# Graph layer in split precision: half of the third batch multiplied whole, and GpSimd's part of the split put in another order

## The reference

```
h   = relu(layernorm(x))                        # 512 x 128
HW_r = h @ W[r, :128] + (W_edges[r] @ W[r, 128:])   # seven relations r
out = max over r of A_r @ HW_r, with A_r in (A, A, roll, A^T, A^T, roll^T, identity)
x   = x + out + b
```

## Time and profile before

| | |
|---|---|
| median of 3 runs | 208.48 us (208.31 to 209.1) |
| the profiled execution | 208.36 us |
| its span in the profile | 206.6 us |
| TensorE busy | 198.2 us (96%), granted clock 1.00 |
| VectorE busy | 178.8 us (87%) |
| ScalarE busy | 162.3 us (79%) |
| GpSimd busy | 130.0 us (63%) |
| mean DMA rate | 247 GB/s |

### The profile page before, as it was taken

One profiled execution on the slowest core, in us unless ns is written; L12 is line 12 of the kernel. 1 busy time (PEld: TensorE's weight loads), 2 busy tenths in 40 slices (PEclk: granted clock), 3 DMA queues, 4 the chain that ended last, 5 costly groups with the idle time before them and its releaser, 6 DMA issues.

```text
span 206.6 us, 3426 instructions
## 1 busy us (share of the span) xinstructions
PE 198.2 (96%) x922; PEld 152.2 (74%) x922; DVE 178.8 (87%) x411; ACT 162.3 (79%) x432; POOL 130.0 (63%) x166
## 2 busy tenths in 40 slices
PE   6999999799999999999999999999999999999991
PEld 6556468568788787878878787877878786887871
DVE  3587869999889998999889998999989999997565
ACT  3987989597979969696997969698896969685230
POOL 4140246969593977939594696919695486959600
PEclk9999999999999999999999999999999999999999
DMA  6999999987896959699795969779695969923201
GB/s 183 311 360 361 361 359 270 304 268 224 312 293 187 387 127 392 153 336 263 244 351 140 389 126 368 218 257 342 210 352 100 396 136 295 261 91 47 65 2 51
DMA packets 33747, 51.07 MB, mean 247 GB/s; under 512 B 1872, under 2 KB 11328, under 8 KB 33728
## 3 DMA queue, kind: packets, MB, share of 16 engines
q1 hardware_dynamic: 31152, 46.53, 66.2%
q0 software_dynamic: 2304, 4.20, 13.1%
q10 hardware_dynamic: 272, 0.13, 0.2%
HBM read 46.65 MB, written 4.19 MB: 246 GB/s over the span
## 4 chain that ended last, share of the span: by engine, by line
PE 70%; DMA 11%; DVE 6%; SPq 4%; POOL 3%; issue 3%; ACT 0%; DVEq 0%; ACTq 0%; POOLq 0%
PE bank_p L846 10%; PE bank_p L847 8%; PE bank_p L848 8%; DMA x_bias<-in_biasT_dram 8%; PE bank_g L809 5%; PE bank_g L811 5%; PE bank_g L817 5%; PE bank_gT L800 5%; PE bank_gT L794 5%; PE bank_gT L791 5%; DMA x_bias<-in_xT_dram 4%; PE bank_p L836 3%; PE bank_p L733 3%; PE bank_p L741 2%; DVE best L632 2%
## 5 line engine op out<-in xcount | busy, mean ns | idle before, releaser
L330 POOL TENSOR_TENSOR a_lo<-adj_sb,a_hi 128x512 fp32r<-128x512 f32 x28 | 36.1, 1310 | 38.0 <-DVE h_lo L601 36.9
L337 POOL TENSOR_TENSOR aT_lo<-adjT_sb,aT_hi 128x512 fp32r<-128x512 f32 x28 | 39.5, 1575 | 0.0
L632 DVE TENSOR_TENSOR best<-bank_p,best 128x512 f32<-128x512 f32 x48 | 33.2, 691 | 5.8 <-PE bank_p L848 4.7
L414 ACT ACTIVATE a_hi<-adj_sb 128x512 fp32r<-128x512 f32 x56 | 34.5, 620 | 0.0
L423 ACT ACTIVATE aT_hi<-adjT_sb 128x512 fp32r<-128x512 f32 x56 | 34.4, 620 | 0.0
L629 DVE SCALAR_TENSOR_TENSOR best<-bank_p,c_col,best 128x512 f32<-128x512 f32 x32 | 23.9, 748 | 5.0 <-ACT best L472 4.4
L595 DVE TENSOR_TENSOR aT_lo<-adjT_sb,aT_hi 128x512 fp32r<-128x512 f32 x28 | 25.4, 945 | 0.0
L435 ACT ACTIVATE h<-x_sb,shift,rstd 128x128 f32<-128x128 f32 x60 | 24.6, 488 | 0.0
L323 POOL TENSOR_TENSOR o_sb<-best,x_bias 128x512 f32<-128x512 f32 x15 | 20.8, 1384 | 3.4 <-DMA x_bias<-in_xT_dram 3.4
L846 PE MATMUL bank_p<-hT_hi,w_hi 128*128 128x512 f32 x48 | 20.1, 420 | 0.4 <-ACT sumsT L465 0.4
L588 DVE TENSOR_TENSOR a_lo<-adj_sb,a_hi 128x512 fp32r<-128x512 f32 x28 | 20.3, 765 | 0.0
(11 more groups left out here) (118 smaller groups left out, 493.9 us busy)
## 6 DMA issues: line engine op xcount, KB each, us to landing
adj_sb<-in_adj_dram SPq DMA_DIRECT2D x15, 1024.0 KB, 5.5
adjT_sb<-in_adjT_dram SPq DMA_DIRECT2D x15, 1024.0 KB, 7.1
x_bias<-in_biasT_dram SPq DMA_DIRECT2D x16, 256.0 KB, 4.8
x_bias<-in_xT_dram POOLq DMA_DIRECT2D x16, 256.0 KB, 5.1
x_sb<-in_x_dram SPq DMA_DIRECT2D x15, 256.0 KB, 7.9
out_dram<-o_sb SPq DMA_DIRECT2D x15, 256.0 KB, 4.1
adj_sb<-in_adj_dram SPq DMA_DIRECT2D x4, 256.0 KB, 4.4
adjT_sb<-in_adjT_dram SPq DMA_DIRECT2D x4, 256.0 KB, 4.8
```

What stands on the lines that cost most here:

```text
L330: nc.gpsimd.tensor_tensor(a_lo[q][:, c, :], adj_sb[q][:, c, :], a_hi[q][:, c, :].bitcast(F32), ALU.subtract).then_inc(alo_last_ready, 1)
L337: nc.gpsimd.tensor_tensor(aT_lo[q][:, c, :], adjT_sb[q][:, c, :], aT_hi[q][:, c, :].bitcast(F32), ALU.subtract).then_inc(aTlo_last_ready, 1)
L414: nc.scalar.activation(a_hi[q][:, c, :], adj_sb[q][:, c, :], ACT.Copy, accum_out=sums[q][:, 0, c:c + 1]).then_inc(ahi_ready, 1)
L632: op = nc.vector.tensor_tensor(best[q][:, :], product, best[q][:, :], ALU.max)
```

## The change

In batch 2, chunks 2 and 3 of both aggregations are multiplied whole in fp32, and chunks 0 and 1 in three passes as before. GpSimd makes no low parts for batch 2. It runs `part_sums(2)` and `add_bias(2)` ahead of its loop, and starts to split at batch 3. In the loop `finish(b - 1)` waits for VectorE's low parts of `aT` of batch b, the split of `a` waits for VectorE's low parts of `a` of the same batch, and `add_bias` goes behind `part_sums`. ScalarE takes `std_of(b + 2)` behind the high parts of `gT` and `hT`. The counts in the loads' waits follow, and the loads also wait for the high parts.

```diff
@@ load_adj, and load_adjT with aThi, aTlo, aTlo_last @@
                 if b >= 2 + FIRST:
+                    sp.wait_ge(ahi_ready, (b - 1 - FIRST) * NS)
                     sp.wait_ge(alo_ready, (b - 1 - FIRST) * ND)
-                    sp.wait_ge(alo_last_ready, (b - 1 - FIRST) * NG)
+                if b > 2 + FIRST:
+                    sp.wait_ge(alo_last_ready, (b - 2 - FIRST) * NG)
@@ gpsimd @@
             add_bias(1)
-            for b in range(1, B):
-                if b >= 2:
-                    finish(b - 1)
+            part_sums(2)
+            add_bias(2)
+            for b in range(2, B):
+
+                pool.wait_ge(aTlo_ready, (b - FIRST + 1) * ND)
+                finish(b - 1)
                 if b + 1 < B:
 
+                    pool.wait_ge(alo_ready, (b - FIRST + 2) * ND)
                     pool.wait_ge(hlo_ready, b - FIRST + 2)
                     split_adj_last(b + 1)
-                    add_bias(b + 1)
                     split_adjT_last(b + 1)
                     part_sums(b + 1)
+                    add_bias(b + 1)
@@ scalar @@
                 if 2 <= b < B - 1:
                     split_adj(b + 1)
+                split_gT(b)
+                split_hT(b)
                 if 2 <= b < B - 2:
                     std_of(b + 2)
-                split_gT(b)
-                split_hT(b)
                 if b + 1 < B:
                     make_h(b + 1)
@@ tensor @@
+            def split_chunks(b):
+
+                return range(ND if b == FIRST else C)
+
             def aggregate_T(b):
                 q = b % 2
                 pe.wait_ge(hhi_ready, b - FIRST + 1)
                 pe.wait_ge(gTlo_ready, b)
-                for c in range(C):
+                if b == FIRST:
+                    pe.wait_ge(adj_in[q], times(b))
+                    for c in range(ND, C):
+                        nc.tensor.matmul(bank_gT[:, 0:N], h[q][:, c, :], adj_sb[q][:, c, :],
+                                         start=(c == ND), stop=False)
+                for c in split_chunks(b):
                     pe.wait_ge(ahi_ready, (b - FIRST) * NS + c + 1)
-                    nc.tensor.matmul(bank_gT[:, 0:N], h_hi[q][:, c, :], a_hi[q][:, c, :], start=(c == 0), stop=False)
+                    nc.tensor.matmul(bank_gT[:, 0:N], h_hi[q][:, c, :], a_hi[q][:, c, :],
+                                     start=(c == 0 and b > FIRST), stop=False)
...
```

More of the change, by code:

```diff
@@ L237, in load_adjT @@
                 if b >= 2 + FIRST:
+                    sp.wait_ge(aThi_ready, (b - 1 - FIRST) * NS)
                     sp.wait_ge(aTlo_ready, (b - 1 - FIRST) * ND)
-                    sp.wait_ge(aTlo_last_ready, (b - 1 - FIRST) * NG)
+                if b > 2 + FIRST:
+                    sp.wait_ge(aTlo_last_ready, (b - 2 - FIRST) * NG)
                 sp.dma_start(adjT_sb[q][:, :, :], adjT_dram[b]).then_inc(adjT_in[q], 16)
@@ L798, in aggregate_T @@
                     else:
-                        pe.wait_ge(alo_last_ready, (b - FIRST) * NG + c - ND + 1)
+                        pe.wait_ge(alo_last_ready, (b - FIRST - 1) * NG + c - ND + 1)
                     last = nc.tensor.matmul(bank_gT[:, 0:N], h_hi[q][:, c, :], a_lo[q][:, c, :],
-                                            start=False, stop=(c == C - 1))
+                                            start=False, stop=(c == split_chunks(b)[-1]))
                 last.then_inc(gT_psum, 1)
@@ L806, in aggregate @@
                 pe.wait_ge(best_done, b * NBEST)
-                for c in range(C):
+                if b == FIRST:
+                    pe.wait_ge(adjT_in[q], times(b))
+                    for c in range(ND, C):
+                        nc.tensor.matmul(bank_g[:, 0:N], h[q][:, c, :], adjT_sb[q][:, c, :],
+                                         start=(c == ND), stop=False)
+                for c in split_chunks(b):
                     pe.wait_ge(aThi_ready, (b - FIRST) * NS + c + 1)
-                    nc.tensor.matmul(bank_g[:, 0:N], h_hi[q][:, c, :], aT_hi[q][:, c, :], start=(c == 0), stop=False)
-                for c in range(C):
+                    nc.tensor.matmul(bank_g[:, 0:N], h_hi[q][:, c, :], aT_hi[q][:, c, :],
+                                     start=(c == 0 and b > FIRST), stop=False)
+                for c in split_chunks(b):
                     nc.tensor.matmul(bank_g[:, 0:N], h_lo[q][:, c, :], aT_hi[q][:, c, :], start=False, stop=False)
-                for c in range(C):
+                for c in split_chunks(b):
                     if c < ND:
@@ L815, in aggregate @@
                     else:
-                        pe.wait_ge(aTlo_last_ready, (b - FIRST) * NG + c - ND + 1)
+                        pe.wait_ge(aTlo_last_ready, (b - FIRST - 1) * NG + c - ND + 1)
                     last = nc.tensor.matmul(bank_g[:, 0:N], h_hi[q][:, c, :], aT_lo[q][:, c, :],
-                                            start=False, stop=(c == C - 1))
+                                            start=False, stop=(c == split_chunks(b)[-1]))
                 last.then_inc(g_psum, 1)
```

## The result

The changed kernel takes 205.41 us (median; 205.12 to 206.52) where the kernel before, timed beside it, takes 208.47. The ratio is 0.9864, with a 95% interval of 0.983 to 0.9898. So it is faster by 1.4%, 3.1 us. The forecast was 205.7 us with a range of 205.0 to 206.9. The profiled execution took 205.48 us with a span of 203.7.

The account below looks back on a forecast made before the run. TensorE's own work was taken to bound the kernel, beside its waits. 208.36 us less 1.91 in batch 2 and 0.88 in later batches gave 205.57, as a median 205.7; range 205.0 to 206.9 us.

Parts of the forecast that it names:

- the two pools: TensorE time to gain beyond its own work: 2.99 us in batch 2 and 0.88 us spread over later batches.
- Items 1 and 3: Batch 2: without GpSimd's split VectorE's pair falls from 3.49 to 1.29 us; the batch takes 12.88, a gain of 1.91.
- Item 2: Batch 2 on TensorE: four whole chunks cost 0.82 us, the passages between split and whole 0.26, together 1.08.
- Items 4 to 6: GpSimd's early part_sums and add_bias and its new loop order cost nothing; all 12 later batches become clean, gaining 0.88 us.
- item 5: GpSimd's order in a clean batch: finish runs T + 3.6 to T + 4.9, just missing VectorE; 1.4 us in hand.
- Item 7: ScalarE's std behind hT_hi leaves sumsT 0.11 us in hand; TensorE's wait taken as 0, bound 1.4 us.
- Rival A: sumsT late for TensorE through std's new place: 0.05 us in 11 batches costs 0.55, giving 206.2 us; chance 0.20.
- Rival D: Slower: late finish holds shift and the pair for a each turn, g_lo passes T + 8.4; 212.7 us; chance 0.06.
- Rival C: Batch 2: another wait replaces the idle time and whole passes eat the rest; at worst 207.6 us; chance 0.08.

Follow-up runs that it names:

- the last group: Changed kernel plus three or six VectorE instructions (batches 2 to 14), two ScalarE ones, or ten VectorE ones in batch 2: 207.84, 213.57, 208.53, 209.1 us.
- the run with one gap: Changed kernel with ten small VectorE instructions (2.15 us) ahead of the low part of g in batch 2 alone: 209.1 us, ratio 1.0009.

## Why the prediction was right

**The bound and the two pools.** TensorE's own work set the time once its waits were gone, and it now fills 94% of the chain. Only the whole chunks leave 142.79 us for the later batches; only the orders leave batch 2 at 15.14. Each pool is opened by one part of the change, as forecast, though the second part alone (208.12 us, interval up to 0.9999) is seen in the trace more than in the time.

**Items 1 and 3.** VectorE's pair took 1.28 us where 1.29 was forecast. Counted from the start of batch 2, all that follows came within 0.3 us of the forecast. The gain in batch 2 was 2.29 us, not 1.91.

**Item 2 is the term that was mis-sized.** It was put at 1.08 us and measured 12.50 - 11.79 = 0.71. From 33.51 to 35.69 run two whole chunks and two passes of 0.23, so a whole chunk takes 0.86 us, not 0.885, and 0.18 more than a split one, not 0.205. The run with all chunks whole gives 0.17. That leaves nearly nothing for the passage from split to whole, for which I had put 0.26. The 0.62 us that I had read for it come from batch 1. In batch 2 the same step took 0.44 us, behind split work (changed kernel) and behind whole work (all chunks whole) alike, so I had taken a figure of batch 1 alone for a price of the passage. Why batch 1 takes longer stays open.

**Items 4 to 6.** `finish` ran from 3.55 to 4.84 us after the batch's start (forecast 3.6 to 4.9) in batch 3, and GpSimd had 1.1 to 1.3 us in hand ahead of it in batches 3 to 13 (forecast 1.4). The later batches gave back 1.00 us, not 0.88. The margin of `g_lo`, wanted 8.4 us after the start, was confirmed from both sides. In the changed kernel it ends at 7.7, as `h_lo` ahead of it waits 0.2 for ScalarE. Three extra instructions were absorbed. With `finish` not held back it ended at 9.14, which is 0.74 over the bound, and the batch took 12.59, 0.8 over a clean one. What item 5 had too small is the move of `add_bias`: it counts its 0.86 us and not the wait for the bias load ahead of it, and put back between the splits it costs 1.3 us (206.73).

**Item 7.** The margin of `sumsT` was 0.16 us (53.37 to 53.53) where I had 0.11, and the signal takes 0.05. Moving `std` back changed nothing. Rival A would have needed more than 0.1 us more.

**Rival D.** Its course, a late `finish` that holds `shift`, was brought about in batch 2 by GpSimd's split behind VectorE's (1.41 us) and, more weakly, with `add_bias` between the splits (0.52). The run with `finish` not held back took 214.1 us, beside the 212.7 that I had worked out, but not in D's way: there `finish` comes early and holds the pair for `aT` (3.06), and `shift` takes its usual 0.16. Only the end is D's, with `g_lo` past 8.4 us. That the two figures lie so near is luck. What the forecast didn't say is that such a collision renews itself from turn to turn, which makes the loss nearly uniform over the batches. Rival C had the right place too. With GpSimd's split of both chunks left in batch 2, another wait does take the idle time's place; with one chunk left to it, or none, no wait does.

**Two misses cancel in part.** The sum had 2.79 us, the trace has 2.89: 0.38 more in batch 2, 0.12 more later, and 0.40 lost ahead of batch 2. The code doesn't explain that last one, and no run was made to explain it. So it is in part luck that the sum and the trace agree to 0.1 us.

## What to carry to other kernels

When two engines hold each other up, read the long instance of a short instruction first. A `shift` of 0.16 us that takes 1.41 tells that the other engine was already inside a long instruction. Tying the long instruction to an event on the other engine places it in a gap. It holds only if the engine comes to that point with time in hand, so move what can wait (here a DMA behind a load) to the end of its turn. Removing one collision by a later start may only move it: follow the late engine to its next instruction, and price extra arithmetic on the bounding engine (0.7 us here) against that.

## What the runs showed of the hardware

Ahead of the tail TensorE's clock fell in one kept trace: after 1.66 us of idle time and 1.5 us of work at full speed, it was granted 0.50 for about 3.4 us. In the tail, behind TensorE's last work, it falls as well and costs nothing: with three more instructions it is 0.50 from 204 us on, and that execution's mean is 0.994. After idle times of 1.45 us and 1.42 us it stayed at 1.00 in the traces that were kept. In the kernel concerned this separates executions of about 207.6 from those of about 209.0 us. A mean clock of 0.982 to 0.990 also stands in 13 of the 61 executions of the kernel before timed beside the experiments, and in 2 of the 12 with only the orders changed. The other ten kernels and the changed one, 72 executions in all, never went below 0.994. No trace shows where the clock fell in those 15, so an idle time of 1.45 us can't be called harmless, and what sets the fall off stays open.

In the four kernels of the last group, all timed on one chip, the passes of the products came every 0.233 us at a granted clock of 1.00, where they came every 0.228 in the others. The passes of the aggregations kept to 0.228 in all (12 of them with 2.74 us, from 69.73 to 72.47, in the run with three more instructions), and ScalarE's and VectorE's instructions kept their times. With 21 such passes in a batch this is the 0.12 us between 11.92 and 11.80, or 1.4 us over the later batches, nearly half of what this change brings. The chip may be the cause, but that isn't shown. The kernel before has executions of 207.57 us on this chip, as fast as the fastest on the other two (207.79 and 208.14). All four kernels also have one more tile, `spare`, declared ahead of the weights, which the products read and the aggregations don't. No trace was kept of a kernel that has the one without the other, so the cause stays open. What makes the comparison sound here is the run with one gap: it has the same tile, and no extra instruction in its later batches.
